# Storing edge counts by whole blocks from one gapless buffer

## The chip, the cores and the metric

The kernel runs on one core of a Trainium2 chip. The metric is device time in microseconds from the start of the program to its end; the time given for a kernel is the median of its runs. Three runs of the kernel before took 2904.08, 2908.68 and 2914.31 us.

## The reference

A graph of 3125 nodes with 256 features each and 53,125 edges (src, dst), sorted by dst, goes through four graph layers. Each is added to its input and normalized over the features:

```python
edge_index = jnp.stack([src, dst])
x = _layernorm(x + _L0_gnn_ref(x, src, dst, ...))   # attention, 8 heads, softmax over the edges of a dst
x = _layernorm(x + _L1_gnn_ref(x, W_lin, W_attn, a, src, dst))
x = _layernorm(x + _L2_gnn_ref(x, src, dst, ...))   # 5 rounds: segment_sum(relu(h[src]), dst), two matmuls
x = _layernorm(x + _L3_gnn_ref(x, edge_index, ...)) # 3 rounds: mean of x[src] over dst, two matmuls

def _L1_gnn_ref(feature, W_lin, W_attn, a, src, dst):
    key = (feature @ W_attn.T).reshape(N, H, D)
    alpha_src = jnp.einsum('nhd,hd->nh', key, a[:, :D])
    alpha_dst = jnp.einsum('nhd,hd->nh', key, a[:, D:])
    score = alpha_src[src] + alpha_dst[dst]
    score = jnp.where(score > 0, score, 0.2 * score)
    ex = jnp.exp(score - segment_max(score, dst)[dst])
    attn = ex / segment_sum(ex, dst)[dst]
    val = (feature @ W_lin.T).reshape(N, H, D)
    return segment_sum(attn[:, :, None] * val[src], dst).reshape(N, OUT_DIM)
```

The last two layers sum features over edges. The kernel does that by matmuls with a dense matrix that holds, for each pair of nodes, the number of edges from one to the other. The second layer makes this matrix on the side.

## The kernel before

The edges are padded to 416 chunks of 128, and 8 chunks make a group, so a layer with attention over edges runs through `NG` = 52 groups. `attend_edges` does this for the first layer (`layer` 0) and the second (`layer` 1). Its code for an engine is one loop over the groups; the step for group g is called a tick. All engines run at once, each through its own program in order, and wait for each other by semaphores only.

A tick of the second layer is made of these parts. GpSimd (POOL) gathers the source rows of the group, 8 indirect DMAs of 128 rows (L827), into one of `RING` = 4 buffers; it may fill a buffer again when TensorE has summed the chunk that lay there four groups earlier (`chunk_summed`, L826). SyncE (SP) reads 8 offsets into registers and issues 8 small DMAs that fetch the windows of destination rows (`load_windows`, L798 to L807). TensorE (PE) spreads the windows (L986), turns scores (L994), turns peaks (L1000) and sums chunks in `sum_parts` (L1016, L1018). VectorE (DVE) makes scores (`take_scores`, L864 to L870), weighs the rows of the group before (L897), scans (L876, L879) and makes one-hot matrices (L841). ScalarE (ACT) takes the sums of each chunk out of PSUM (L1119, L1121) and makes exponentials (L1100, L1101).

The edge counts come beside this, in the first 50 ticks. The matrix is cut by destination into `NBLOCK` = 8 blocks of `AN` = 391 columns, and the columns are counted in windows of 5. 640 windows make 160 groups of four windows, so 3 or 4 groups (3.2 on the mean) fall to a tick. VectorE makes two one-hot matrices for them (`spot_windows`, L929 and L931); TensorE multiplies these (L1031); ScalarE copies the 128 x 500 counts of a group from PSUM to the SBUF tile `counts` in f16 (`copy_counts`, L1134). A block of 391 columns has a first half of 200 columns and a second half of 191; ten groups fill a half, some three ticks. `counts` holds two halves, 25 (`NT`) rows of 200 columns per partition for each. When a half is full, four ticks after its last group was made, SP issues a DMA that stores it to the matrix `adj` in HBM (`store_halves`, L788 to L796), behind the window loads of that tick and on the same queue. In HBM a partition of a block holds 25 rows of 391 columns without a gap, so a half is stored as 3200 runs of 400 or 382 bytes. ScalarE waits for the store of a half before it writes that half again (L1130), and SP waits for the last two stores at the end (L817).

When all engines are through, the stage ends with a barrier; a short check for repeated edges follows, and then the normalization (`merge_norm`) begins, where the first loads of `adj` are issued too. Its first VectorE instruction is L2122.

The columns `count_ps` of a group lie in PSUM by window, row and column (w, t, j). In the stage VectorE's `slots` operand lies in PSUM as well (`e_fixed`).

Of the kernel before, what the change touches and what calls it, by code (L numbers as in the profile page):

```python
# [7 lines left out]
F16 = mybir.dt.float16  # L8
# [3 lines left out]
ACT = mybir.ActivationFunctionType  # L12
AX_X = mybir.AxisListType.X

P = 128
# [4 lines left out]
NT = -(-N // P)  # L20
# [35 lines left out]
WIN = 5  # L56
# [649 lines left out]
def attend_edges(nc, keep, layer, by_src, by_part, ws, wd, scale, adj=None, begun=None):  # L706
# [7 lines left out]
    with Phase(nc) as ctx:  # L714
# [20 lines left out]
        if counting:  # L735

            WT, TICKS = 4 * WG, NG - 2
            is_place = sb("is_place", [P, 2, WT, P], F16)
            is_key = sb("is_key", [P, 2, WT, NT * WIN], F16)
            counts = sb("counts", [P, 2, NT, HALF], F16)  # L740
        PAIRS = G // 2
# [34 lines left out]
        spotted, counted, copied = sems(nc, ctx, *(f"e{layer}_{n}" for n in ("spotted", "counted", "copied")))  # L776
        half_out = sems(nc, ctx, *(f"e{layer}_half_out{i}" for i in range(2)))
        block = ctx.enter_context(nc.Block(f"edges{layer}"))
# [3 lines left out]

        def width_of(half):
            return AN - HALF if half % 2 else HALF

        @block.sync
        def _(sp):
            def store_halves(g):  # L788

                for half in range(NHALF):  # L790
                    done = next(t for t in range(NG) if HG * (half + 1) <= NWG * (t + 1) // TICKS)
                    if g == min(NG - 1, done + 4):
                        sp.wait_ge(copied, HG * (half + 1))
                        at = half % 2 * HALF
                        sp.dma_start(adj[half // 2][:, :, at:at + width_of(half)],
                                     counts[:, half % 2, :, 0:width_of(half)]).then_inc(half_out[half % 2], 16)  # L796

            def load_windows(it, b, again):  # L798
# [12 lines left out]
            for g in range(RING, NG):  # L811
                load_windows(g // RING, g % RING, True)
                if counting:
                    store_halves(g)
            if counting:
                for i in range(2):
                    sp.wait_ge(half_out[i], 16 * (NHALF // 2))  # L817

# [13 lines left out]
        def _(v):  # L832
# [69 lines left out]
            def tick(g):  # L902
# [16 lines left out]
                if ahead:  # L919
                    match(g + 1, 3)  # L920

            def spot_windows(g):
# [164 lines left out]
        def _(act):  # L1087
# [37 lines left out]
            def copy_counts(g, first, last):  # L1125

                for q in groups_of(g)[first:last]:
                    half, at = q // HG, q % HG * WG * WIN
                    if q % HG == 0 and half >= 2:
                        act.wait_ge(half_out[half % 2], 16 * (half // 2))  # L1130
                    act.wait_ge(counted, q + 1)
                    of = count_ps[q % 2][:, 0:WG * NT * WIN].rearrange("p (w t j) -> p t w j", w=WG, t=NT)
                    to = counts[:, half % 2, :, at:at + WG * WIN].rearrange("p t (w j) -> p t w j", w=WG)
                    nc.scalar.activation(to, of, ACT.Identity, scale=keep["whole"][:, 0:1]).then_inc(copied, 1)  # L1134

            def tick_rows(g):
# [5 lines left out]
                copy_sums(g - 1, (3,))  # L1142

            def tick_alpha(g):
                copy_sums(g - 2, range(4, G))
                copy_counts(g - 1, 0, 1)
                copy_sums(g - 1, (0, 1))
                copy_counts(g - 1, 1, 2)
                if g + 2 < NG:
                    copy_turned(g + 2)  # L1150
                copy_sums(g - 1, (2,))
                copy_counts(g - 1, 2, 3)
                weigh(g)
                copy_sums(g - 1, (3,))
                copy_counts(g - 1, 3, 4)
# [1994 lines left out]
```

## Time and profile before

| what | value |
|---|---|
| runs | 2904.08, 2908.68, 2914.31 us, median 2908.68 |
| profiled execution | 2904.07 us, of which the span is 2902.3 us |
| busy share of the span | PE 91%, DVE 53%, ACT 38%, POOL 34% |
| DMA | 332,504 packets, 470.20 MB; 155,942 packets under 512 B |
| the edge stage of the second layer | from some 830 us to 1372.8 us of the span |

The page gives busy times over the whole span, and the mean over stages with different limits says little about one of them. The chain on the page that ended last goes back through the last layer alone (19% of the span) and does not reach the edge stage. So the stage has to be read by itself: busy times in stretches, waits within it, and the order of single instructions. "DMA share" is the mean busy share of the 16 DMA engines. An idle time ends with its releaser, `<-`; "issue" is time in which the engine waited for nothing that the profile shows.

### The profile page before, as it was taken

To read this page: it belongs to the slowest core of one execution; us is meant where nothing else is said; L and a number is where in the kernel's file an instruction comes from. 1 tells how busy PE (TensorE), PEld (TensorE's weight loads), DVE (VectorE), ACT (ScalarE), POOL (GpSimd) and SP (SyncE) were. 2 spreads that over 40 slices of the span, in tenths; PEclk is the share of its full clock that TensorE was granted. 3 is DMA by queue.
4 is the path that set the end of the run, shared out by engine and by line. 5 is a ranking of instruction groups with operands and counts; after the bars stand their busy time and mean duration, and the time that the engine had idled before them with its cause. 6 is when DMAs were issued, how large, how long until landed. Compare 5 with 4: busy or idle time off the path is not lost. (4 is left out here: it accounts for less than half of the span.)

```text
span 2902.3 us, 53181 instructions
## 1 busy us (share of the span) xinstructions
PE 2627.4 (91%) x17158; PEld 1910.1 (66%) x17158; DVE 1546.9 (53%) x2779; ACT 1106.6 (38%) x3027; POOL 973.4 (34%) x1020
## 2 busy tenths in 40 slices
PE   6789999998747888877799999999999989999998
PEld 4679999996636777776455555555555566565654
DVE  8589999996457988886712414124141251111123
ACT  1145555554346777776312304023040252111111
POOL 3577777773477777773400101001010000000000
PEclk8999999999869999999799999999999999999999
DMA  7799999992348898896554342533415133434342
GB/s 261 254 320 321 315 316 318 316 313 96 99 103 142 152 151 158 154 153 107 162 163 115 105 126 63 164 113 105 133 55 165 43 127 111 140 89 132 114 122 86
DMA packets 332504, 470.20 MB, mean 162 GB/s; under 512 B 155942, under 2 KB 243062, under 8 KB 331588
## 3 DMA queue, kind: packets, MB, share of 16 engines
q1 hardware_dynamic: 269364, 286.33, 38.0%
q0 software_dynamic: 59088, 176.67, 19.9%
q10 hardware_dynamic: 3776, 3.80, 0.4%
q8 instruction: 139, 2.28, 0.3%
q14 instruction: 137, 1.12, 0.1%
HBM read 412.95 MB, written 55.50 MB: 161 GB/s over the span
## 5 line engine op out<-in xcount | busy, mean ns | idle before, releaser
L2368 PE MATMUL sum_ps<-room,high 128*128 128x391 f16 x1900 | 469.3, 330 | 2.4 <-DVE z_t L2545 2.4
L2368 PE MATMUL sum_ps<-room,low 128*128 128x391 f16 x1824 | 453.5, 330 | 0.0
L827 POOL DMA_INDIRECT e_from_src<-vk,src x416 | 394.4, 948 | 140.7 <-issue 108.9
L827 POOL DMA_INDIRECT rows<-val,src x410 | 388.8, 948 | 134.7 <-issue 102.8
L2766 PE MATMUL sum_ps<-room,high 128*128 128x391 f16 x1200 | 389.4, 329 | 0.5 <-DVE x L2910 0.5
L2766 PE MATMUL sum_ps<-room,low 128*128 128x391 f16 x1152 | 379.3, 329 | 0.0
L1016 PE MATMUL e_part_ps<-e_onehot,rows 128*128 128x129 f32 x1664 | 289.3, 298 | 77.6 <-ACT ends L1121 69.3
L2545 DVE SCALAR_TENSOR_TENSOR z_t<-h_t,own,sum_ps 128x391 f32<-128x391 f32 x80 | 44.7, 617 | 482.4 <-PE sum_ps L2368 478.7
L1016 PEld LDWEIGHTS e_part_ps<-e_onehot,rows 128*128 128x128 f32 x1664 | 226.1, 197 | 105.7 <-ACT ends L1121 94.5
L1119 ACT ACTIVATE sums<-e_part_ps 128x384 f32 x416 | 205.5, 494 | 227.9 <-PE e_part_ps L1018 201.6
L2436 POOL TENSOR_SCALAR h_t<-h_t 128x391 f32<-128x391 f32 x32 | 39.0, 1237 | 693.8 <-DVE h_t L2575 693.8
L1016 PE MATMUL e_part_ps<-x,e_from_src 128*128 128x129 f32 x1664 | 267.0, 283 | 1.7 <-DVE e_from_src L897 1.2
L2368 PEld LDWEIGHTS sum_ps<-room,high 128*128 128x128 f16 x1900 | 184.9, 98 | 125.9 <-issue 3.0
L2368 PEld LDWEIGHTS sum_ps<-room,low 128*128 128x128 f16 x1824 | 177.9, 98 | 127.1 <-issue 1.6
L2445 ACT ACTIVATE gin_y_t<-gin_proj_ps,gin_columns 128x391 f32<-128x391 f32 x80 | 47.0, 588 | 559.7 <-PE gin_proj_ps L2385 558.9
L1119 ACT ACTIVATE room<-e_part_ps 128x384 f32 x416 | 206.5, 496 | 135.6 <-PE e_part_ps L1018 70.4
L1016 PEld LDWEIGHTS e_part_ps<-x,e_from_src 128*128 128x128 f32 x1664 | 229.7, 191 | 20.0 <-DVE e_from_src L897 2.1
L986 PE MATMUL e_spread_ps<-e_window,x 128*128 128x256 f32 x832 | 214.6, 385 | 14.9 <-DMA e_window<-q_part 14.8
L2766 PEld LDWEIGHTS sum_ps<-room,high 128*128 128x128 f16 x1200 | 116.8, 97 | 80.3 <-issue 1.2
L986 PEld LDWEIGHTS e_spread_ps<-e_window,x 128*128 128x128 f32 x832 | 144.5, 193 | 33.5 <-DMA e_window<-q_part 12.4
L850 DVE TENSOR_TENSOR e_from_src<-e_from_src,e_spread_ps 128x512 f32<-128x512 f32 x208 | 139.6, 671 | 49.2 <-PE e_spread_ps L986 47.3
L2766 PEld LDWEIGHTS sum_ps<-room,low 128*128 128x128 f16 x1152 | 112.3, 97 | 80.4 <-issue 2.1
(424 smaller groups left out, 4558.3 us busy)
## 6 DMA issues: line engine op xcount, KB each, us to landing
room<-adj SPq DMA_DIRECT2D x128, 977.5 KB, 4.9
e_window<-q_part SPq DMA_DIRECT2D x416, 128.0 KB
room<-adj SPq DMA_DIRECT2D x32, 488.8 KB
room<-adj SPq DMA_DIRECT2D x32, 391.0 KB
adj<-e_counts SPq DMA_DIRECT2D x8, 1250.0 KB
adj<-e_counts SPq DMA_DIRECT2D x8, 1193.8 KB
e_from_src<-vk,src POOLq DMA_INDIRECT x416, 4.5
rows<-val,src POOLq DMA_INDIRECT x416
```

The source lines that it names most:

```text
L827: nc.gpsimd.indirect_dma_start(from_src[:, b, j, :], None, by_src, bass.IndirectOffsetOnAxis(ap=keep["src"][:, g * G + j:g * G + j + 1], a ...
L850: nc.vector.tensor_tensor(k_rows, k_rows, spread_ps[pair % 2][:, :].rearrange("p (j d) -> p j d", j=2), ALU.mult).then_inc(used[pair % 2], 1)
L986: mm = nc.tensor.matmul(to, onehot_t[:, r, j, :], window[:, r, j, :], start=True, stop=True)
L1016: nc.tensor.matmul(part_ps[s][:, k * ENDS:(k + 1) * ENDS], from_src[:, b, j, k * P:(k + 1) * P], onehot[:, b, j, :], start=True, stop=True)
L1119: nc.scalar.activation(keep["sums"][:, :, bass.ds(starts[j], P)], of[:, :, 0:P], ACT.Copy).then_inc(whole_copied, 1)
L2368: mm = nc.tensor.matmul(sum_ps[KH * n + m][:, 0:AN], part[:, t, m * P:(m + 1) * P], slab[s][:, n, k * AN:(k + 1) * AN], start=(t == 0 and ...
L2436: nc.gpsimd.tensor_scalar(h_t[:, 1, cols(b)], h_t[:, 1, cols(b)], 0.0, None, ALU.max).then_inc(floored, 1)
L2445: nc.scalar.activation((z_t if p else y_t)[:, m, cols(b)], proj_bank(p, v)[:, 0:AN], ACT.Identity, bias=columns[:, 3 * p, m:m + 1], scale= ...
L2545: nc.vector.scalar_tensor_tensor(out=z_t[:, m, cols(b)], in0=h_t[:, m, cols(b)], scalar=own[:, l:l + 1], in1=sum_ps[KH * n + m][:, 0:AN], ...
L2766: mm = nc.tensor.matmul(sum_ps[KH * n + m][:, 0:AN], part[:, t, m * P:(m + 1) * P], slab[s][:, n, k * AN:(k + 1) * AN], start=(t == 0 and ...
```

## The change

`counts` becomes one buffer of whole rows, 25 x 391 columns per partition, without a gap. The first halves are collected apart, in `counts_head` (25 x 200). VectorE copies a full `counts_head` into the first 200 columns of each row of `counts`, in one instruction at the end of its tick (`move_heads`), two ticks after the tick of the half's last group, and after the store of the block before has landed. ScalarE writes the second halves straight into columns 200 to 390 of `counts`; the last group of a second half has 11 columns, written by two instructions (two windows, then one column). Before, that group was written by one instruction of 20 columns, of which 11 were stored. When both halves are there, ScalarE issues the store of the block itself, as one DMA, at the start of its tick (`store_blocks`); in HBM and in SBUF the 25 x 391 elements of a partition now lie without a gap. SP has no stores any more and waits for all eight at the end.

With 3.2 groups to a tick, the eight copies come at the ends of VectorE's ticks 5, 11, 17, 23, 30, 36, 42 and 48, and the eight stores at the starts of ScalarE's ticks 8, 14, 20, 26, 33, 39, 45 and 51, the last tick.

```diff
-            counts = sb("counts", [P, 2, NT, HALF], F16)
+            counts_head = sb("counts_head", [P, NT, HALF], F16)
+            counts = sb("counts", [P, NT, AN], F16)
...
-            def store_halves(g):
-
-                for half in range(NHALF):
-                    done = next(t for t in range(NG) if HG * (half + 1) <= NWG * (t + 1) // TICKS)
-                    if g == min(NG - 1, done + 4):
-                        sp.wait_ge(copied, HG * (half + 1))
-                        at = half % 2 * HALF
-                        sp.dma_start(adj[half // 2][:, :, at:at + width_of(half)],
-                                     counts[:, half % 2, :, 0:width_of(half)]).then_inc(half_out[half % 2], 16)
...
+        def last_tick(half):
+            return next(t for t in range(NG) if HG * (half + 1) <= NWG * (t + 1) // TICKS)
...
             if counting:
-                for i in range(2):
-                    sp.wait_ge(half_out[i], 16 * (NHALF // 2))
+                sp.wait_ge(block_out, 16 * NBLOCK)
...
+                if counting:
+                    move_heads(g)
+
+            def move_heads(g):
+
+                for b in range(NBLOCK):
+                    if g == last_tick(2 * b) + 2:
+                        v.wait_ge(copied, HG * (2 * b + 1))
+                        if b:
+                            v.wait_ge(block_out, 16 * b)
+                        nc.vector.tensor_copy(counts[:, :, 0:HALF], counts_head[:, :, :]).then_inc(head_moved, 1)
...
-                    if q % HG == 0 and half >= 2:
-                        act.wait_ge(half_out[half % 2], 16 * (half // 2))
+                    b, whole = half // 2, keep["whole"][:, 0:1]
+                    of = count_ps[q % 2][:, 0:WG * NT * WIN].rearrange("p (w t j) -> p t w j", w=WG, t=NT)
+                    if half % 2 == 0:
+                        if q % HG == 0 and b:
+                            act.wait_ge(head_moved, b)
+                        to = counts_head[:, :, at:at + WG * WIN].rearrange("p t (w j) -> p t w j", w=WG)
+                        act.wait_ge(counted, q + 1)
+                        nc.scalar.activation(to, of, ACT.Identity, scale=whole).then_inc(copied, 1)
+                        continue
+                    if q % HG == 0 and b:
+                        act.wait_ge(block_out, 16 * b)
+                    n = min(WG * WIN, AN - HALF - at)
+                    wins, rest = n // WIN, n % WIN
+                    lo = HALF + at
+                    to = counts[:, :, lo:lo + wins * WIN].rearrange("p t (w j) -> p t w j", w=wins)
                     act.wait_ge(counted, q + 1)
-                    of = count_ps[q % 2][:, 0:WG * NT * WIN].rearrange("p (w t j) -> p t w j", w=WG, t=NT)
-                    to = counts[:, half % 2, :, at:at + WG * WIN].rearrange("p t (w j) -> p t w j", w=WG)
-                    nc.scalar.activation(to, of, ACT.Identity, scale=keep["whole"][:, 0:1]).then_inc(copied, 1)
+                    done = nc.scalar.activation(to, of[:, :, 0:wins, :], ACT.Identity, scale=whole)
+                    if rest:
+                        done = nc.scalar.activation(counts[:, :, lo + wins * WIN:lo + n], of[:, :, wins, 0:rest], ACT.Identity, scale=whole)
+                    done.then_inc(copied, 1)
...
+            def store_blocks(g):
+
+                for b in range(NBLOCK):
+                    if g == last_tick(2 * b + 1) + 2:
+                        act.wait_ge(copied, HG * (2 * b + 2))
+                        act.wait_ge(head_moved, b + 1)
+                        act.dma_start(adj[b].rearrange("p t c -> p (t c)"), counts[:, :, :].rearrange("p t c -> p (t c)")).then_inc(block_out, 16)
+
             def tick_alpha(g):
+                store_blocks(g)
                 copy_sums(g - 2, range(4, G))
```

## Rows read from the trace of the kernel before

**Rows 1.** Windows: length, busy us (xcount) of PE, PEld, DVE, ACT, POOL, PEclk, DMA share, GB/s.
```profile
860.00:890.00 30.00, 25.33 (x236) 22.48 (x234) 26.79 (x38) 22.10 (x67) 22.72 (x24) 0.94 0.49 115
...
1040.00:1070.00 30.00, 26.15 (x242) 23.25 (x240) 25.86 (x37) 22.84 (x68) 22.69 (x25) 0.94 0.90 155
```

**Rows 2.** Timeline of POOL: start, us, line, and idle time before.
```profile
912.87 0.95 POOL L827 DMA_INDIRECT rows<-val,src  x1 [0.30 <-issue]
917.45 0.95 POOL L827 DMA_INDIRECT rows<-val,src  x1 [3.63 <-PE e_part_ps L1018]
920.12 0.94 POOL L827 DMA_INDIRECT rows<-val,src  x1 [1.72 <-PE e_part_ps L1018]
921.73 0.95 POOL L827 DMA_INDIRECT rows<-val,src  x1 [0.66 <-PE e_part_ps L1018]
...
1327.82 0.95 POOL L827 DMA_INDIRECT rows<-val,src  x1 [0.30 <-issue]
...
1337.86 0.94 POOL L827 DMA_INDIRECT rows<-val,src  x1 [0.31 <-issue]
```

**Rows 3.** Waits, 830 to 1375 us: us in total, times, longest.
```profile
POOL rows L827 <- PE e_part_ps L1018: 27.1, 72, 3.6
PE e_turn_ps L986 <- DMA e_window<-alpha_part: 21.2, 11, 8.4
DVE e_spread_score L864 <- DMA rows<-val,src: 11.5, 11, 2.3
```

**Rows 4.** Timeline of SP's queue: start, us, line, merged issues.
```profile
824.07 67.66 SPq L807 DMA_DIRECT2D e_window<-alpha_part  x64
891.77 0.62 SPq L795 DMA_DIRECT2D adj<-e_counts  x1
899.71 23.05 SPq L807 DMA_DIRECT2D e_window<-alpha_part  x24
922.80 0.57 SPq L795 DMA_DIRECT2D adj<-e_counts  x1
...
1352.22 0.55 SPq L795 DMA_DIRECT2D adj<-e_counts  x1
```

**Rows 5.** Timeline of DVE: the first score instruction of a tick, and the next stage.
```profile
940.66 0.34 DVE L864 TENSOR_REDUCE e_spread_score<-e_turn_ps 128x64 f32<-128x192 f32 x1
949.95 0.34 DVE L864 TENSOR_REDUCE e_spread_score<-e_turn_ps 128x64 f32<-128x192 f32 x1
...
1342.21 0.36 DVE L864 TENSOR_REDUCE e_spread_score<-e_turn_ps 128x64 f32<-128x192 f32 x1
1347.90 0.35 DVE L864 TENSOR_REDUCE e_spread_score<-e_turn_ps 128x64 f32<-128x192 f32 x1
...
1372.81 0.06 DVE L2122 MEMSET h_t<- 8x1 f32 x1 [11.39 <-PEq L79]
```

**Rows 6.** Waits of SP's own queue, 830 to 1400 us.
```profile
SPq L817 <- DMA adj<-e_counts: 11.9, 1, 11.9
```

**Rows 7.** DMA issues: count, KB each, median us to landing; then one issuing line.
```profile
pr_x_t<-in_x_t SPq DMA_DIRECT2D x1, 3200.0 KB, 23.1
out<-pr_zero SPq DMA_DIRECT2D x5, 642.5 KB, 3.6
L586 ACTq DMA_DIRECT2D q_part<-pr_part_room x4: 378/378/433, 94.6 to 124.1; - x4
```

**Rows 8.** VectorE instructions: two SBUF casts (ns min/median/max), one kind of L931.
```profile
L370 DVE CAST pr_ints<-pr_counts x1: 370/370/370, 13.4 to 13.4; 128x416 int32<-128x416 f32 x1
L472 DVE CAST pr_dst_pair<-pr_low x1: 474/474/474, 78.0 to 78.0; 128x640 f32<-128x640 int32 x1
L931 DVE TENSOR_TENSOR e_is_key<-e_fixed,key_t 128x1500 f16<-128x1500 f32 x32 | 54.4, 1701 | 0.0
```

**Rows 9.** Timelines near 690 and 770 us: an indirect DMA beside a VectorE instruction.
```profile
690.18 1.01 DVE L1472 TENSOR_SCALAR m_factor<-m_factor 8x1664 f32<-8x1664 f32 x1
690.78 1.27 POOL L1568 DMA_INDIRECT out<-m_rows,part_index  x1 [0.62 <-issue]
...
769.24 1.48 DVE L1685 TENSOR_TENSOR x<-x,n_more 128x1280 f32<-128x1280 f32 x1
769.72 1.83 POOL L1670 DMA_INDIRECT alpha_parts<-alpha,alpha_index  x1 [0.30 <-issue]
```

More of the change, by code:

```diff
@@ L776, in attend_edges @@
         spotted, counted, copied = sems(nc, ctx, *(f"e{layer}_{n}" for n in ("spotted", "counted", "copied")))
-        half_out = sems(nc, ctx, *(f"e{layer}_half_out{i}" for i in range(2)))
+        block_out, head_moved = sems(nc, ctx, f"e{layer}_block_out", f"e{layer}_head_moved")
         block = ctx.enter_context(nc.Block(f"edges{layer}"))
@@ L781, in groups_of @@
             return range(NWG * g // TICKS, NWG * (g + 1) // TICKS) if 0 <= g < TICKS else range(0)
-        def width_of(half):
-            return AN - HALF if half % 2 else HALF
+        def last_tick(half):
+            return next(t for t in range(NG) if HG * (half + 1) <= NWG * (t + 1) // TICKS)
         @block.sync
         def _(sp):
-            def store_halves(g):
-                for half in range(NHALF):
-                    done = next(t for t in range(NG) if HG * (half + 1) <= NWG * (t + 1) // TICKS)
-                    if g == min(NG - 1, done + 4):
-                        sp.wait_ge(copied, HG * (half + 1))
-                        at = half % 2 * HALF
-                        sp.dma_start(adj[half // 2][:, :, at:at + width_of(half)],
-                                     counts[:, half % 2, :, 0:width_of(half)]).then_inc(half_out[half % 2], 16)
             def load_windows(it, b, again):
@@ L812, in _ @@
                 load_windows(g // RING, g % RING, True)
-                if counting:
-                    store_halves(g)
             if counting:
-                for i in range(2):
-                    sp.wait_ge(half_out[i], 16 * (NHALF // 2))
+                sp.wait_ge(block_out, 16 * NBLOCK)
         @block.gpsimd
```

## The prediction

> **What bounds the kernel now.** I read the edge stage by stretches first, since the page's shares mix stages. From 860 to 890 us, before any store, and at 1040 to 1070 us, with stores, POOL issues the same 24 to 25 gathers in 30 us; the DMA share is 0.49 in the one and 0.90 in the other [rows 1]. No engine is full: VectorE 25.9 to 26.8 of 30 us, TensorE 25 to 26, ScalarE 22 to 23. POOL is not full by its busy time either (22.7), but its timeline shows a gather of 0.95 us every 1.25 us with 0.30 us between, the spacing of its own issue [rows 2]. From 1327.82 to 1337.86 us eight gathers take 10.04 us. So POOL sets the pace: 10.04 us for a tick, whatever the DMA engines do.
>
> POOL falls behind this pace in one place. At 912.87 us a gather starts in step; the next ones start after idle times of 3.63, 1.72 and 0.66 us instead of 0.30, a loss of 3.33 + 1.42 + 0.36 = 5.1 us [rows 2]. In the table of waits, POOL's waits for TensorE come to 27.1 us in 72 times; without these three that is 21.1 in 69, the normal 0.30 each [rows 3]. The releaser is a chunk sum, and TensorE was late because it had waited for windows: up to 8.4 us in one wait [rows 3]. The first store was issued at 891.77 us on the queue on which the windows come, and the next window load followed at 899.71 [rows 4]. So the first store cost 5.1 us.
>
> The stores also wear on what comes behind the gathers. Eight sets of window loads without a store took SP 67.7 us, 8.5 per set; from a store to the next, with three sets, it takes 31.0 us [rows 4], a little more than POOL's three ticks (30.1). VectorE waits for gathered rows 11 times, 11.5 us [rows 3]. VectorE can go faster than POOL where it is behind: from tick to tick 9.3 us [rows 5]. Yet it starts tick 50 at 1342.21 us, 13.4 us after the last gather of that tick ended (1327.82 + 0.95), and tick 51 at 1347.90, 9.1 us after the last gather of all (1337.86 + 0.94) [rows 2, 5]. The stage ends when this backlog is worked off: 1372.81 us is 30.6 us after the start of tick 50 [rows 5]. The last store is no part of it: SP's wait for it is 11.9 us [rows 6] and starts at 1352.8 [rows 4], so it is over at 1364.7, eight us before the stage's end.
>
> **The change part by part.**
>
> *The stall at the first store goes: -5.1 us.* SP issues windows only, at 8.5 us for a set against 10.04 us per tick, so it stays ahead, and the windows no longer queue behind 3200 short runs. The bounds: nothing is won if the large store on the same DMA engines delays the windows as much, and 5.1 us is all that POOL lost. I take the upper end, since SP's own time is then out of it. What is late next is POOL's own issue, which nothing here makes shorter.
>
> *The backlog at the end shrinks: -5 us.* Small runs cannot hold up the rows of tick 50 any more, since the last store is issued at the start of ScalarE's tick 51; and one store for six ticks stands where there were two. The end can't come earlier by more than 9.1 us, tick 51's own distance from its last gather [rows 2, 5], and may gain nothing if the ticks keep their distance. If tick 50 came down to the 9.1 us that tick 51 shows, that were 4.3 us. VectorE, with 9.3 us against 10.04, has some forty ticks in which to catch up, so I take 5, near the middle of 0 and 9.1.
>
> *The eight copies on VectorE.* Such a copy (5000 f16 elements per partition, SBUF to SBUF) is not in the trace. Bounds for one: the casts of 4-byte elements in SBUF take 370 ns for 416 and 474 for 640 [rows 8], that is 0.46 ns for one more, and with 0.18 us of fixed time 2.5 us; if 2-byte elements go by bytes, 0.23 ns and 1.3 us. From the other side, L931 writes f16 at 1.13 ns each [rows 8]: 5.7 us. I take 1.5 us, nearest to the casts by bytes. As VectorE time this is 0.24 us per tick, beside 0.7 us of slack (10.04 - 9.3), and hides behind POOL's gathers; at 5.7 us it would be 0.9 and would not hide (a rival below). Queued behind a copy is the next tick's score, for which TensorE waits (L994). Its wait for `copied` and for the last block's store was met long before: the store is three ticks older.
>
> *The copies hold up gathers: +7 us.* Here is what hides nothing. Twice the trace shows an indirect DMA of POOL that started while VectorE worked on SBUF alone. At 769.72 us one took 1.83 us; VectorE's instruction ended at 770.72, 0.83 us before the DMA. At 690.78 one took 1.27; VectorE's ended at 691.19, 0.86 before [rows 9]. A free gather takes 0.95. So a gather that starts beside such an instruction waits, from about 0.1 us after its start, until that one ends. The second VectorE instruction has one SBUF input, as a copy has. In the edge stage VectorE's long instructions read PSUM, and the gathers are even [rows 2]. With a copy of 1.5 us and gathers every 1.25, the first gather to start within it loses between 0.25 and 1.5 us, 0.87 on the mean; eight copies make 7 us, on the engine that sets the pace. Bounds: 0, if this copy does not hold gathers, and 15, with copies of 2.5 us (8 x (2.5 - 0.63)). The Trainium skill (SBUF — State Buffer, Who interferes with whom) has this as a rule: a VectorE copy in a mode that uses two ports shuts GpSimd out for the whole instruction, and the one that starts second waits. The rows above agree, with 1.27 and 1.83 for 0.95 us. On the price only a page speaks: by the skill (VectorE: DVE Perf Modes, The perf-mode tier table) a 16-bit copy in SBUF goes at four elements a cycle, 693 ns for 2048, which makes an estimate of 1.5 us for 5000 and would leave the sum as it is.
>
> *ScalarE issues the stores: +1 us.* A DMA issue takes ScalarE 0.38 us [rows 7] and SP's stores took 0.55 to 0.62 [rows 4]; before it ScalarE waits for its own last copy, some 0.7 us. The first seven lie in ticks in which ScalarE is busy 22.8 of 30 us [rows 1]: nothing. What is queued behind are the sums of the group before last, for which TensorE waits; that is a delay of 1 us with POOL two groups ahead. The eighth stands in front of the end's backlog, where ScalarE works without pause: +1 us, between 0.4 and 1.2.
>
> *The stores themselves.* A block is 2444 KB. 642.5 KB landed in 3.6 us, 3200 KB under load in 23.1 [rows 7]; in proportion, a block takes 14 to 18 us, under a fixed share less. The last one, issued about where SP's last store is now (1352.22 [rows 4]), 20.6 us before the stage's end, is then through in time or just so; cost 0, at most 3. The others have three ticks. The split of the last group into two instructions and the direct write to longer rows change ScalarE's count by 8 of some 3000: nothing.
>
> **Sum** against the profiled execution (2904.07 us, the span of 2902.3 and 1.8 around it): -5.1 - 5 + 7 + 1 = -2.1, thus 2902. This execution lies 4.6 us under the median of 2908.68, the measure for the result; there the sum gives 2906.6. I predict 2906.5.
>
> **Rivals.**
>
> *The copies do not hold gathers* (or hardly): without the +7 it is -9.1, 2899.6 us. For it: the two rows are few, and only one has a single SBUF input. Against it: both waits end alike, 0.83 and 0.86 us after VectorE.
>
> *The copies are long* and VectorE becomes the bound: slower. At 5.7 us each, one in 6.25 ticks, a tick takes 9.5 (9.3, and 1.1 more in each fifth tick, which has four groups) + 0.9 = 10.4 us. VectorE's tick 10 starts at 940.66 us [rows 5]; without the first stall that were 8 us less (5.1 and some 3 of TensorE's own), and forty such ticks end at 1348.6, against 1342.21: +6.4, and 1 us for ScalarE: 2916. It decides from where a copy takes 3.4 us (0.54 us of slack x 6.25). With two elements a cycle (2.5 us) the hold of 15 us does nearly the same: -5.1 - 5 + 15 + 1 = +5.9, 2914.6. Against both: by bytes it is 1.3 us.
>
> *The first stall stays*, as the windows queue behind large runs on the same engines: 5.1 more, 2911.6. Against it: a partition's row is one run, and there are 128 of them instead of 3200.
>
> *The store isn't spread over the DMA engines*, as it should be: with one of 16, 977 KB and more would take far over the 60 us between stores, VectorE and ScalarE would wait for it each time, and some hundreds of us come on top. Against it: `out<-pr_zero`, also gapless on one side, landed 642.5 KB in 3.6 us [rows 7].
>
> **How the numbers follow.** Likeliest, as summed: 0.52. No hold: 0.26. Long copies or long holds: 0.12. First stall stays: 0.08. Not spread: 0.02. 0.3% is 8.7 us, about what a measurement can tell from no change. Within it lie most of the sum's own cases (0.44 of 0.52; 0.06 faster, 0.02 slower), a third of no hold (0.08, 0.18 faster), a third of the long ones (0.04, 0.08 slower) and nearly all of the stall (0.07, 0.01 slower). Faster 0.24, same 0.63, slower 0.13. The range goes from no hold with the full 9.1 at the end (-13.2: 2895) to the long copies and a little over (2918).
>
> **What would show it.** Gathers longer than 0.95 us, eight of them by 0.3 to 1.5, beside the copies at ticks 5, 11 and so on; no gap over 0.4 us in POOL near 915 us; a copy near 1.5 us; tick 50's score under 10 us after its last gather; a DMA share well under 0.9. I am wrong if the gathers stay even (faster), if copies take over 3 us, if windows are waited for, or if SP's last wait ends the stage.

## The result and the profile after

The changed kernel takes 2916.99 us (median; 2912.91 to 2920.76), 1.0033 times the kernel before on the same chip (95% interval 1.0021 to 1.0044): by that ratio 9.6 us slower. Forecast were 2906.5 us and a gain of 2 us.

The profiled execution has a span of 2915.2 us, 12.9 more than before. Ahead of the edge stage lie 3.7 of these (VectorE's first instruction of the stage is at 823.24 us, before at 819.57), behind it -0.7; both vary from run to run (819.6 to 827.4 us in the traces below) and the change does not touch them. The stage itself, from that instruction to VectorE's leaving it (1370.1 us before, 1383.7 after, each 2.7 us ahead of the next stage's first MEMSET), grew from 550.5 to 560.4 us: +9.9. From here on this is "the stage". It splits at the end of POOL's last gather: 519.2 + 31.3 us before, 523.2 + 37.2 after. Lines have moved (L827 is L815, L864 is L852, L986 is L985).

The two stretches of [rows 1], same columns:

```profile
860.00:890.00 30.00, 25.43 (x236) 22.57 (x236) 26.75 (x37) 22.74 (x70) 22.70 (x24) 0.95 0.49 115
1040.00:1070.00 30.00, 25.01 (x223) 22.04 (x222) 24.66 (x37) 20.37 (x65) 21.33 (x24) 0.89 0.64 191
```

The DMA share with stores fell from 0.90 to 0.64, as forecast, but all engines did less work in the 30 us than before, POOL too (21.33 for 22.69). Something behind the gathers holds them up. POOL's timeline at the first store (start, us, line, idle before), then the last gather of tick 50 and the last of all:

```profile
916.44 0.94 POOL L815 DMA_INDIRECT rows<-val,src  x1 [0.31 <-PE e_part_ps L1017]
917.69 0.96 POOL L815 DMA_INDIRECT rows<-val,src  x1 [0.30 <-issue]
918.96 0.95 POOL L815 DMA_INDIRECT rows<-val,src  x1 [0.30 <-issue]
...
1335.50 0.95 POOL L815 DMA_INDIRECT rows<-val,src  x1 [0.30 <-issue]
...
1345.51 0.95 POOL L815 DMA_INDIRECT rows<-val,src  x1 [0.30 <-issue]
```

The stall of [rows 2] is gone, and no gather is longer than 1.0 us. The waits from 830 to 1390 us (total, times, longest), against [rows 3]:

```profile
POOL rows L815 <- PE e_part_ps L1017: 43.3, 110, 1.7
DVE e_fixed L864 <- PE e_turn_ps L993: 42.6, 43, 2.9
PE e_turn_ps L985 <- DMA e_window<-alpha_part: 10.8, 3, 5.3
```

Waits for windows halved (21.2 to 10.8, what is left lies at the stage's start) and those of VectorE for rows are gone from the list. But POOL's waits for TensorE, 27.1 us before, are 43.3: many small ones in place of one large. VectorE shows where they come from. Its copy (duration in ns: least, median, most), then the first score instruction of ticks around a copy and at the end, against [rows 5]:

```profile
L919 DVE COPY e_counts<-e_counts_head x8: 2737/2740/2742, 895.2 to 1339.5; 128x5000 f16<-128x5000 f16 x8
```

```profile
1010.05 0.34 DVE L852 TENSOR_REDUCE e_spread_score<-e_turn_ps 128x64 f32<-128x192 f32 x1
...
1019.35 2.74 DVE L919 COPY e_counts<-e_counts_head 128x5000 f16<-128x5000 f16 x1
1022.01 0.34 DVE L852 TENSOR_REDUCE e_spread_score<-e_turn_ps 128x64 f32<-128x192 f32 x1
...
1030.51 0.34 DVE L852 TENSOR_REDUCE e_spread_score<-e_turn_ps 128x64 f32<-128x192 f32 x1
...
1351.69 0.34 DVE L852 TENSOR_REDUCE e_spread_score<-e_turn_ps 128x64 f32<-128x192 f32 x1
1359.09 0.35 DVE L852 TENSOR_REDUCE e_spread_score<-e_turn_ps 128x64 f32<-128x192 f32 x1
...
1386.36 0.06 DVE L2144 MEMSET h_t<- 8x1 f32 x1 [11.38 <-PEq L79]
```

The copy takes 2.74 us, not 1.5. A tick with one takes 12.0 us (1010.05 to 1022.01) against POOL's 10.04; the next 8.5. Tick 50 starts 15.2 us after its last gather (13.4 before), tick 51 12.6 (9.1).

There is a second place. ScalarE issues the store at the start of a tick. Its offset loads in the 9 us before one store and in the 9 us from it (ns as above), and its timeline there:

```profile
L1108 ACTq TENSOR_LOAD <-offset x7: 275/277/285, 1032.0 to 1041.1; - x7
```

```profile
L1108 ACTq TENSOR_LOAD <-offset x6: 285/876/1232, 1042.2 to 1049.1; - x6
```

```profile
1041.88 0.33 ACTq L1163 DMA_DIRECT2D adj<-e_counts  x1
1042.16 0.17 ACT L1120 ACTIVATE ends<-e_part_ps 128x6 f32<-128x6 f32 x1
1044.06 0.49 ACT L1118 ACTIVATE room<-e_part_ps 128x384 f32 x1 [1.73 <-PE e_part_ps L1017]
...
1050.37 0.49 ACT L1118 ACTIVATE room<-e_part_ps 128x384 f32 x1 [1.80 <-issue]
```

The issue is 0.33 us, as forecast. But while the 2.4 MB run (8.1 to 8.8 us to the last packet; 6.8 for the last store), a load of one offset takes up to 1.23 us, 0.88 in the middle, instead of 0.28, and behind such loads stand the sums for which TensorE waits, and then VectorE's scan. The 42.6 us of the scan's waits above are no proof of it: the kernel before has 40.0. The two ticks from a store on take 21.3 to 22.5 us together, where two plain ones take 18.6, or 19.6 if four groups are counted in one of them.

### The profile page after: what moved, and what is told of

Read it like the earlier page. It is cut to its first block and busy times, and to the rows that moved or that the text cites. A ratio compares the mean times of both kernels' runs of the same rounds, so it can differ in the third digit from the quotient of the medians.

```text
span 2915.2 us, 53203 instructions
## 1 busy us (share of the span) xinstructions
PE 2646.0 (91%) x17158; PEld 1923.4 (66%) x17158; DVE 1566.4 (54%) x2787; ACT 1107.9 (38%) x3035; POOL 971.4 (33%) x1020
## 3 DMA queue, kind: packets, MB, share of 16 engines
q1 hardware_dynamic: 217908, 266.31, 31.1%
## 5 line engine op out<-in xcount | busy, mean ns | idle before, releaser
L815 POOL DMA_INDIRECT e_from_src<-vk,src x416 | 393.8, 947 | 141.4 <-issue 107.0
L815 POOL DMA_INDIRECT rows<-val,src x410 | 388.1, 947 | 139.4 <-issue 91.2
L2390 PEld LDWEIGHTS sum_ps<-room,low 128*128 128x128 f16 x1824 | 177.7, 97 | 126.6 <-issue 0.7
L985 PE MATMUL e_spread_ps<-e_window,x 128*128 128x256 f32 x832 | 216.5, 388 | 13.3 <-DMA e_window<-q_part 11.9
L985 PEld LDWEIGHTS e_spread_ps<-e_window,x 128*128 128x128 f32 x832 | 145.9, 195 | 31.9 <-DMA e_window<-q_part 12.3
L1017 PE MATMUL e_part_ps<-e_onehot,e_small 128*65 128x129 f32 x832 | 166.9, 284 | 0.0
```

The costliest lines, as they stand in the source:

```text
L815: nc.gpsimd.indirect_dma_start(from_src[:, b, j, :], None, by_src, bass.IndirectOffsetOnAxis(ap=keep["src"][:, g * G + j:g * G + j + 1], a ...
L985: mm = nc.tensor.matmul(to, onehot_t[:, r, j, :], window[:, r, j, :], start=True, stop=True)
L1017: nc.tensor.matmul(part_ps[s][0:SMALL, KH * ENDS:(KH + 1) * ENDS], small[:, r, j, :], onehot[:, b, j, :], start=True, stop=True).then_inc( ...
L2390: mm = nc.tensor.matmul(sum_ps[KH * n + m][:, 0:AN], part[:, t, m * P:(m + 1) * P], slab[s][:, n, k * AN:(k + 1) * AN], start=(t == 0 and ...
```

## Experiments

Theory A: the copies cost by their time on VectorE. Theory B: the store costs where ScalarE issues it. Rival C: the transfer itself. Later also: do the prices overlap, with POOL as a floor, or add? Ratios are to the kernel before on the same chip; the stage and its split are read from one trace each. The two measures agree within some 4 us, but for the store after the sums (7 us).

| kernel | ratio (95% interval) | stage | to last gather | rest |
|---|---|---|---|---|
| before | 1 | 550.5 | 519.2 | 31.3 |
| after | 1.0033 (1.0021 to 1.0044) | 560.4 | 523.2 | 37.2 |
| no copy | 0.9989 (0.9976 to 1.0001) | 546.4 | 513.2 | 33.2 |
| store mid-tick | 1.0052 (1.0031 to 1.0072) | 564.2 | 530.2 | 34.0 |
| rows of 392 | 1.0045 (1.0027 to 1.0064) | 560.6 | 523.9 | 36.7 |
| SyncE's store | 0.9995 (0.9982 to 1.0008) | 550.0 | 516.5 | 33.5 |
| neither | 0.9937 (0.9924 to 0.9949) | 535.3 | 513.0 | 22.3 |
| 5 groups apart | 0.9979 (0.9968 to 0.9990) | 546.8 | 512.9 | 33.9 |
| loads ahead | 1.0014 (0.9999 to 1.0029) | 555.1 | 518.8 | 36.3 |
| 5 groups, loads ahead | 0.9967 (0.9955 to 0.9980) | 542.0 | 513.1 | 28.9 |
| 5 groups, SyncE early | 1.0119 (1.0091 to 1.0147) | 589.3 | 558.2 | 31.1 |
| store after sums | 0.9995 (0.9979 to 1.0011) | 556.0 | 520.4 | 35.6 |
| copy twice | 1.0082 (1.0060 to 1.0104) | 573.0 | 537.1 | 35.9 |
| 4-byte pairs | 1.0033 (1.0020 to 1.0046) | 561.0 | 526.3 | 34.7 |
| padded input | 0.9984 (0.9970 to 0.9999) | 548.0 | 522.8 | 25.2 |
| 6 groups, SyncE | 0.9955 (0.9937 to 0.9974) | 541.2 | 512.9 | 28.3 |
| 6, SyncE, padded | 0.9962 (0.9947 to 0.9976) | 541.3 | 519.5 | 21.8 |

**No copy.**

```diff
+    rows = NT if b == 0 else 1
-    nc.vector.tensor_copy(counts[:, :, 0:HALF], counts_head[:, :, :])
+    nc.vector.tensor_copy(counts[:, 0:rows, 0:HALF], counts_head[:, 0:rows, :])
```

> The changed kernel, but VectorE moves the first half of block 0 whole and of blocks 1 to 7 one row of 25 (so the first halves of seven blocks are wrong in 24 rows). All waits, stores and ScalarE's work stay. Theory A (the copies set the time: each is 2.74 us on VectorE, whose ticks are 9.3 us and 12.0 after a copy, against 10.04 us for eight gathers): seven copies lose 2.6 us each, 18 us of VectorE, and POOL's spacing sets the pace again without the first store's stall: the stage falls by 9 to 13 us, 2904 to 2908 us, POOL's waits for TensorE fall from 43 us to under 30. Theory B (what costs is ScalarE's part: its offset loads take 0.85 to 1.45 us instead of 0.27 while its own store runs, some 2.5 us in each of eight store ticks): 0 to 3 us less, 2914 to 2917.

The stage fell by 14.0 us, 1 us over the expected range, 2.0 for each of seven copies: the copy's tick is 2.6 us shorter (9.4 for 12.0), the next one 0.7 longer. Theory A holds; POOL's waits for TensorE are 28.8 us.

**The store in the middle of ScalarE's tick.**

```diff
 def tick_alpha(g):
-    store_blocks(g)
...
     copy_counts(g - 1, 1, 2)
+    store_blocks(g)
```

> The changed kernel, but ScalarE issues the block's store in the middle of its tick (behind the second group of counts, ahead of the turned one-hot rows) and not at the start, ahead of the sums of chunks 4 to 7 for which TensorE waits. Theory A: no change beyond 2 us, 2915 to 2919. Theory B: the five offset loads at the start of the tick run before the store at 0.27 us each and five fewer are slowed; up to 2.5 us in each of eight ticks, 2900 to 2910.

Neither: 3.8 us longer. VectorE's first score instructions of ticks 33 to 35; the store, at 1182.44 us, is in tick 33:

```profile
1176.00 0.34 DVE L852 TENSOR_REDUCE e_spread_score<-e_turn_ps 128x64 f32<-128x192 f32 x1
1185.30 0.34 DVE L852 TENSOR_REDUCE e_spread_score<-e_turn_ps 128x64 f32<-128x192 f32 x1
1199.09 0.34 DVE L852 TENSOR_REDUCE e_spread_score<-e_turn_ps 128x64 f32<-128x192 f32 x1
```

The store's tick costs nothing (9.3 us), as B said, but the next one pays 13.8 (12.2 to 13.8 behind the first seven stores): the transfer, 10.5 us long here, to 1192.9, covers that tick's start, where the loads stand ahead of the sums. So the place counts, and this one is worse.

**Rows of 392 columns in the store's buffer.**

```diff
-counts = sb("counts", [P, NT, AN], F16)
+counts = sb("counts", [P, NT, AN + 1], F16)
...
+    counts[:, :, :].rearrange("p t c -> p (t c)")[:, 0:NT * AN]   # what is stored
```

> The changed kernel, but a row of the store's buffer in SBUF has 392 columns instead of 391, so that each row of the copy's output starts at an even element; the store takes the first 9775 elements of a partition, as gapless as before (the counts in memory are displaced by one column more from row to row). If the odd rows keep the copy at two elements a cycle, it falls from 2.74 to about 1.4 us. Theory A then gives back half of the copies, 8 x 1.3 = 10.7 us of VectorE: 2907 to 2911, unless the faster copy holds gathers (which would then show 0.3 to 1.4 us over 0.95 beside the copies). If the copy stays at 2.74 us, both theories say no change, 2915 to 2919. Theory B: no change in either case.

The copy stayed at 2.74 us, the stage at 560.6: rows that begin at an odd element are not what makes it slow.

**SyncE issues the block's store.**

```diff
 for g in range(RING, NG):
     load_windows(g // RING, g % RING, True)
+    store_blocks(g)     # with sp.dma_start, where g == min(NG - 1, last_tick(2 * b + 1) + 4)
```

> The changed kernel, but the block's store is issued by SyncE, on the queue of the window loads, at the place that the halves' stores had; the gapless buffer and the copies stay. Theory A: the copies still set the time, 2914 to 2920. Theory B in the form that the issue on ScalarE is what costs: 5 to 15 us less, 2902 to 2912. Theory B in the form that the transfer slows the loads whoever issues it: about 2917, with slow offset loads on ScalarE as before, and windows that are waited for up to some us behind the store.

10.4 us less, and windows are waited for no more than in the kernel after (10.6 us). ScalarE's loads are still slowed (31 over 0.4 us, 39 in the kernel after), so the slowing as such is not the price; where the loads fall in the tick is the more likely one. The scan's waits for TensorE fell from 42.6 us to 30.5:

```profile
DVE e_fixed L874 <- PE e_turn_ps L1003: 30.5, 42, 2.6
```

SyncE's first seven stores start 0.0 to 2.8 us after a score. Those at 2.0 and over leave the two ticks at 19.6 to 20.4 us; those at 0.0 to 1.3 still cost 20.6 to 21.6. The granted TensorE clock in four stretches from 850 to 1350 us was 0.93 to 0.95 here and 0.91 to 0.99 in the kernel after, so the clock does not explain the difference.

**Neither.** Both edits together, the copies of seven blocks left out and SyncE's store.

```diff
+    nc.vector.tensor_copy(counts[:, 0:rows, 0:HALF], counts_head[:, 0:rows, :])
...
+    store_blocks(g)     # on SyncE's queue
```

> No copies (seven of eight moved in one row of 25 only, so the first halves of seven blocks are left out in 24 rows) and the block's store issued by SyncE: both edits that took the loss away each by itself. The stage from VectorE's first instruction took 550.5 us before, 560.4 after, 546.4 without copies, 550.0 with SyncE's store. Theory: VectorE with its copies (2.0 us net per copy) and ScalarE with its slowed loads make the consumers slower than POOL's 10.04 us per tick, each alone hardly does, so the two prices (14.0 and 10.4 us) overlap and don't add: the stage ends with POOL again, 543 to 547 us, the whole 2896 to 2902. Rival: the prices add, as two waits on one chain: stage 536 us, 2890 to 2893.

The theory of a floor fell: 535.3, where the rival said 536. From the kernel after, 14.0 and 10.4 us alone, 25.1 together (by the ratios 12.8, 11.0 and 27.9). POOL's last gather came before 512.9 us in no run, but the rest shrank from 33 to 22.3 us. VectorE's score of the last tick, and the next stage (the last gather ended at 1332.89):

```profile
1335.55 0.36 DVE L862 TENSOR_REDUCE e_spread_score<-e_turn_ps 128x64 f32<-128x192 f32 x1 [2.79 <-DMA rows<-val,src]
...
1357.95 0.06 DVE L2146 MEMSET h_t<- 8x1 f32 x1 [11.39 <-PEq L79]
```

Here the scores wait for rows, 2.7 us after the last gather. In the kernel before that distance is 9.1 us [rows 2, 5] and after the change 12.6: there the engines behind the gathers were late.

**Five of twenty groups apart.**

```diff
+HEADS, WHOLE = 5, 2 * HG
-    if half % 2 == 0:            # into counts_head
+    if q % WHOLE < HEADS:
```

> The changed kernel, but only the first 5 of a block's 20 groups of counts (100 of 391 columns) are collected apart and moved; ScalarE still issues the store. The copy is then 2500 elements, about 1.4 us instead of 2.74 if it goes by elements. If the copies' time on VectorE is the cause, half of their price of 14 us is won back and perhaps more, stage 550 to 554 us, 2904 to 2909 us. If what costs is a wait that comes with the copy (for the store before it, or the second half's counts behind it), the stage stays at 558 to 562 or grows: 2913 to 2920.

The copy takes 1.44 us, and the stage is that of no copies (0.4 us more), 3 us better than the best expected. Half the copy costs next to nothing, though the copies also come at other ticks here.

**Offsets of a store's tick loaded a tick ahead.**

```diff
+def hold(g, chunks):
+    for j in chunks:
+        held[g, j] = act.value_load(keep["offset"][0:1, bass.ds(g * G + j, 1)], ...)
...
+    if stored_next:
+        hold(g - 1, range(4, G))      # and hold(g, range(4)) behind the next sum
```

> The changed kernel, but ScalarE loads the eight offsets of a store's tick in the tick before, ahead of the store, so that none of its loads in that tick runs beside the transfer; the loads are as many as before. Theory B (the loads, 0.85 to 1.45 us beside a transfer and 0.27 else, delay the sums for which TensorE and then the scores wait): the first tick of a store falls from 10.3 to 11.4 us to 9.3 to 10.3 and the second, which is late by it, to near 9.5; 1 to 2.5 us for each of eight stores, stage 548 to 553, 2903 to 2909. Rival C (the transfer itself takes the DMA engines or SBUF from the gathered rows and windows): no change, stage 558 to 562, 2914 to 2919.

ScalarE's loads, held ones first, 840 to 1390 us:

```profile
L1106 ACTq TENSOR_LOAD <-offset x64: 273/275/287, 912.1 to 1355.3; - x64
L1116 ACTq TENSOR_LOAD <-offset x352: 270/276/295, 846.9 to 1373.6; - x176
```

None is slow any more, and the second tick of a store falls to 8.7 to 9.8 us. The scan's waits for TensorE fall to 30.1 us here too. But the tick before has eight loads more, in two rows of four, the first seven stores come 1.9 to 4.4 us after the score instead of 0.9 to 2.0, and a store's tick takes 9.7 to 13.6. Net 5.3 us of 10.4: short of the 7 to 12 expected, and not nothing, as C had it. What the rest is stays open.

**Five groups and loads ahead.**

```diff
+HEADS, WHOLE = 5, 2 * HG
...
+        hold(g - 1, range(4, G))
```

> Five groups apart and the offsets of a store's tick loaded ahead. If both causes are right, the consumers are faster than POOL in all ticks but the copies', and the stage ends with POOL as without copies: 544 to 548 us, 2898 to 2903, faster than before by 0.1 to 0.35%. If loading ahead does nothing, it is as with five groups alone.

542.0 us, 2 us better than the best expected: the two gains add here too.

**Five groups, SyncE's store.** Five groups apart, with the run of SyncE's store, but the store stood two sets of windows earlier in SyncE's queue than in the run of SyncE's store, which the expectation did not reckon with.

```diff
-    if g == min(NG - 1, last_tick(2 * b + 1) + 4):
+    if g == last_tick(WHOLE * (b + 1)) + 2:
```

> Five of twenty groups collected apart (copies of 2500 elements, 1.44 us) and the block's store issued by SyncE. The run without both costs had a stage of 535.3 us against 546.4 and 550.0 with one of them: the prices add, so VectorE, TensorE and ScalarE behind the gathers set the time and not POOL. With five groups and ScalarE's store the stage was 546.8, 0.4 us over no copies at all. If prices add, this one has 535 to 538 us, 2889 to 2894, faster than before by 0.4 to 0.6%. If POOL's gathers, which end 513 us after the stage's start at the earliest, set the time from there, or the windows on SyncE's queue do, it stays near 544 to 547, 2899 to 2903.

589.3 us. TensorE's waits for windows (total, times, longest):

```profile
PE e_turn_ps L997 <- DMA e_window<-alpha_part: 48.4, 11, 11.3
```

SyncE waits at the store for the counts, 72.1 us in eight waits, and the windows stand behind it. It says nothing on five groups, but shows what a wait on that queue costs.

**The store behind ScalarE's first sums.**

```diff
 def tick_alpha(g):
-    store_blocks(g)
     copy_sums(g - 2, range(4, G))
+    store_blocks(g)
```

> The changed kernel, but ScalarE issues the block's store behind the first four sums of its tick (chunks 4 to 7 of the group before last), with copies as they are. SyncE's stores, 2.0 to 2.8 us after the tick's scores, left the two ticks at 19.4 to 20.6 us together; ScalarE's at 0.9 us gave 21.1 to 22.5, at 6.4 us 22 to 23. If the place in the tick is what costs (slowed loads ahead of the sums that TensorE's turning of the scores waits for), this store, some 3 to 4 us after the scores, comes near SyncE's: stage 550 to 556 us, 2904 to 2911. If the issue from ScalarE is what costs, wherever it stands: 559 to 564, 2914 to 2921.

By the median it comes level with SyncE's store; in the trace only 4.4 us of 10.4 are gone (556.0, the upper end). So the place is at least part of it; whether the rest lies in ScalarE is left open by these two measures.

**Copy twice.** The buffer is first copied onto itself (L919), then moved (L921).

```diff
+nc.vector.tensor_copy(counts_head[:, :, :], counts_head[:, :, :]).then_inc(doubled, 1)
+v.wait_ge(doubled, b + 1)
 nc.vector.tensor_copy(counts[:, :, 0:HALF], counts_head[:, :, :]).then_inc(head_moved, 1)
```

> The changed kernel, but VectorE copies the buffer of the first halves onto itself before each move, eight copies more of 5000 elements. If copies cost by their time on VectorE (14 us for seven less, 2.0 us net each of 2.74), eight more cost 16 to 24 us: stage 576 to 585, 2931 to 2940. If the first copy only takes up what was idle and a wait set its price, eight more cost under 6 us, 2917 to 2923.

The copy onto itself took 1.45 us where 2.74 had been reckoned, for as many elements:

```profile
L919 DVE COPY e_counts_head<-e_counts_head x8: 1445/1448/1449, 892.3 to 1350.5; 128x5000 f16<-128x5000 f16 x8
L921 DVE COPY e_counts<-e_counts_head x8: 2757/2757/2758, 893.8 to 1352.0; 128x5000 f16<-128x5000 f16 x8
```

Eight of 1.45 make 11.6 us; the stage grew by 12.6, less than expected only as these copies were short. On top of a copy of 2.74 us VectorE's time goes straight into the stage; a copy of 1.44 us by itself did not (five groups). And the fast copy does what the slow one doesn't:

```profile
1018.74 1.98 POOL L815 DMA_INDIRECT rows<-val,src  x1 [0.30 <-issue]
1019.15 1.45 DVE L919 COPY e_counts_head<-e_counts_head 128x5000 f16<-128x5000 f16 x1
1020.63 2.76 DVE L921 COPY e_counts<-e_counts_head 128x5000 f16<-128x5000 f16 x1
1021.03 0.96 POOL L815 DMA_INDIRECT rows<-val,src  x1 [0.30 <-issue]
```

One gather is held by each of the eight (1.86 to 2.23 us for 0.95), in three of them one that had started before the copy.

**The same bytes as 4-byte pairs**, in rows of 392.

```diff
+nc.vector.tensor_copy(counts[:, :, :].bitcast(F32)[:, :, 0:HALF // 2], counts_head[:, :, :].bitcast(F32))
```

> The run with rows of 392 columns (2.74 us per copy, stage 560.6 us), but the same bytes are moved as 2500 4-byte elements instead of 5000 of 2 bytes. By the casts of 4-byte elements (0.46 ns for one more) a copy would take 1.3 us, and at one such element a cycle 2.7. If it falls to 1.3 to 1.5 us and the copies' time is the cause, the stage falls by 5 to 11 us, to 550 to 556, 2904 to 2911, with gathers at 0.95 us if the copy holds none. If it stays at 2.7 us, no change: 2914 to 2920.

```profile
L921 DVE COPY e_counts<-e_counts_head x8: 2739/2741/2747, 893.1 to 1339.0; 128x2500 f32<-128x2500 f32 x8
```

Half the elements, the same 2.74 us: the second outcome.

```diff
-counts_head = sb("counts_head", [P, NT, HALF], F16)
+counts_head = sb("counts_head", [P, NT, HALF + 2], F16)
...
+    nc.vector.tensor_copy(counts[:, :, 0:HALF], counts_head[:, :, 0:HALF])
```

> The changed kernel, but a row of the first halves' buffer is 202 columns long instead of 200, so that the copy reads 25 rows of 200 and writes 25 rows of 200. In the changed kernel's trace it reads one run of 5000 and writes 25 rows, 2.74 us; the copy of the buffer onto itself, one run to one run, took 1.45 us and lengthened a gather by 0.9 to 1.3 us. If it is the unlike shape that halves the rate, the copy now takes 1.45 us and each copy holds one gather. The copies' net price then falls by 8 x 1.3 = 10 us, stage 549 to 553 us, 2903 to 2908, if a held gather costs nothing (POOL waits for the rest of the engines 10.8 us anyway); if POOL sets the pace, the holds give back 8 x 1.1 = 9 us: 558 to 561, 2913 to 2917. If rows alone halve the rate, the copy stays at 2.74 us and nothing changes.

```profile
L919 DVE COPY e_counts<-e_counts_head x8: 1497/1498/1499, 892.3 to 1326.4; 128x5000 f16<-128x5000 f16 x8
```

```profile
1012.13 1.99 POOL L815 DMA_INDIRECT rows<-val,src  x1 [0.30 <-issue]
1012.60 1.50 DVE L919 COPY e_counts<-e_counts_head 128x5000 f16<-128x5000 f16 x1
1014.42 0.94 POOL L815 DMA_INDIRECT rows<-val,src  x1 [0.30 <-issue]
```

Two columns that nothing uses halve the copy. Each copy now holds one gather, 9.0 us in all (1.84 to 2.47 for 0.947), which moves POOL's last gather to 522.8; yet the stage is 12.4 us shorter, since VectorE was the later one: it is 1.6 us over the stage without copies. The Trainium skill (Advanced Engine Details and Errata, 2x-2p Requirements) has a rule for the fast form that agrees: the outermost dimension must be even in input and output, or odd and equal; 5000 against 25 is neither, 25 against 25 is. No run here varied whether a count is even.

**Six groups and SyncE's store in its old place**, and **the same with padded rows** (122 columns for 120).

```diff
+HEADS, WHOLE = 6, 2 * HG
...
+    if g == min(NG - 1, last_tick(WHOLE * (b + 1)) + 4):     # on SyncE's queue
...
+counts_head = sb("counts_head", [P, NT, HEAD + 2], F16)     # the second run only
```

> Six of twenty groups apart (copies of 3000 elements, 1.7 us) and the store issued by SyncE behind the windows of the same tick as in the first run with SyncE's store; the run with five groups had it two sets of windows earlier, ahead of the counts being done, and its windows waited 11 us in each store. If the prices add: 535 to 539 us of stage, 2889 to 2894, faster than before by 0.45 to 0.65%. If SyncE's store with fewer groups apart still comes too late for the block's seventh group, ScalarE waits for it: 545 us and more, over 2900.

> The same with rows of 122 columns for the 120 that are copied, so that the copy runs in the fast form, if that is what the shape decides: 0.9 us instead of 1.7. VectorE gains 6 us, but in this run POOL's last gather, not VectorE, should be what the stage ends with, and eight gathers are held by up to 1 us each: -3 to +5 us against the run without the padding.

541.2 us (2895.14 as a whole): 2 us over the expectation, and faster than both kernels, by 0.45% than before. With padded rows the copy is 0.96 instead of 1.70 us and holds eight gathers for 5.5 us together: 541.3, no difference. What VectorE wins POOL loses, as expected.

## Why the prediction was wrong

**The step that failed** is "The eight copies on VectorE": "I take 1.5 us [...] and hides behind POOL's gathers". It measured 2.74 us, and it did not hide: the eight cost 14.0 us, where nothing was reckoned. The size was right for a copy of like shapes (1.45 and 1.50 us); the change's copy has unlike ones. Of that size copies do hide, nearly: 1.44 us cost 0.4 us of stage, 1.50 us 1.6. With 1.50 us the same kernel took 2904.7 us, 0.9984 of the time before, against the 2906.5 forecast; 12.4 us of stage hang on this term. That nearness does not bear out every term: to the last gather that run has +3.6 (forecast -5.1 + 7 = +1.9), behind it -6.1 (forecast -5 + 1 = -4), and of ScalarE's store, which cost 10.4 us beside the long copies, at most 2.9 are left at its end (25.2 against 22.3). The signs named beforehand missed the case: gathers at 0.95 us were to mean faster, and the copies stayed under 3 us.

**The reading under it failed too**: "So POOL sets the pace". POOL was even, but because it may run ahead. The engines behind it were 9 to 13 us late at the end, and that lateness is the stage's end. Taking both costs out brought the end to 22 us after the last gather, and what was added on VectorE to a copy of 2.74 us came out at the end (copy twice). The 0.7 us of slack per tick was reckoned from 9.3 us ticks; [rows 5] show one such tick; from tick 10 to tick 50 the same rows give (1342.21 - 940.66) / 40 = 10.04 us, no less than POOL's pace, and single ticks of the kernel before go up to 14.7. In the kernel after the mean is 10.30. So "it decides from where a copy takes 3.4 us" was too high: 2.74 was enough, and 1.5 was near the limit.

**First stall, -5.1**: right as to the stall. No gather is longer than 1.0 us and windows are waited for at the stage's start only; where nothing else holds POOL, the last gather is 513 us after the start, 6 before the old one. In the changed kernel the engines behind hold POOL, and it is 523.2.

**Backlog, -5**: wrong sign, +5.9. The bound of 9.1 was right: without copies and ScalarE's store it is 31.3 - 22.3 = 9.0.

**Held gathers, +7**: 0, as the slow form holds none. In the fast form eight gathers lost 9.0 us, so the hold of [rows 9] was read rightly and placed on the wrong copy. One detail differs: in five of those eight the gather had started 0.2 to 0.6 us before the copy and was held all the same, so that here it is not always the one that starts second that waits.

**ScalarE's issue, +1**: 10.4 us. The issue is 0.33 us, and what stands behind it was counted; that ScalarE's offset loads are slow while a store runs was not, though the loads of the kernel before show it too (42 of 416 over 0.4 us). That the place of the store costs is shown by SyncE's store; that it does so by the loads is shown for 5.3 us (loads ahead), and the rest is open.

**The stores themselves, 0**: right, 6.8 to 8.8 us each (14 to 18 were forecast), done before they were waited for.

As a balance: without either cost the stage is 535.3. The kernel before stands 15.2 over it (6.2 to the last gather, 9.0 behind). The change takes that away and puts 14.0 for copies and 11.1 for ScalarE's store in its place (546.4 - 535.3): 25.1 - 15.2 = +9.9. This closes by construction, as every price is a difference of two stages; in the other order, SyncE's store first, the prices are 10.4 and 14.7. The forecast had -10.1 and +8.

The rival of long copies named the sign and nearly the time (2916), by way of VectorE. But it had copies of 5.7 us for that, and they took 2.74, with ScalarE's store beside them: that the time came so near is luck. Its other form, held gathers, did not occur.

## What to carry to other kernels

An engine with an even rhythm that may run ahead is not yet the bound: look how far the engines behind it are late, and whether that lateness shrinks where nothing disturbs. Before pricing a copy, write down both access patterns as they are encoded, with merged runs; a few columns of padding halved it here, and the faster form then held up GpSimd. A DMA issue is cheap, but price what its engine has to load from memory while the transfer runs, and put it where the next such load is far away.

## What was not expected of the hardware

A copy of 5000 2-byte elements per partition took 2.74 us from one run to 25 rows, 1.50 from 25 rows to 25 rows and 1.45 from one run to one; as 2500 4-byte elements from one run to 25 rows again 2.74. In the slow form it made no difference whether a row began at an even element. Only the fast ones lengthened an indirect DMA of GpSimd beside them, by 0.9 to 1.5 us, also where it had started up to 0.66 us before.

While a transfer of 2.4 MB out of SBUF ran (some 8.4 us), loads of one value into a register took up to 1.45 us instead of 0.28 on ScalarE and up to 1.43 instead of 0.27 on SyncE in the changed kernel, and up to 1.41 and 1.36 with SyncE's store: they were slow on both engines, whichever of the two had issued the transfer.
